# Expert results summed by an accumulating scatter into four arrays, and a combine that reads four rows per token

## The reference

```python
TOP_K = 8
shared = jax.nn.silu(xf @ Ws_up) @ Ws_down
aff = xf @ centroids.T                        # 64 experts
_, idx = jax.lax.top_k(aff + expert_biases, TOP_K)
w = jax.nn.sigmoid(jnp.take_along_axis(aff, idx, axis=1))
w = w / (jnp.sum(w, axis=-1, keepdims=True) + 1e-08)
cw = jnp.zeros((T, E)).at[jnp.arange(T)[:, None], idx].add(w)
h = jax.nn.silu(jnp.einsum('td,edf->etf', xf, W_up))
y = jnp.einsum('etf,efd->etd', h, W_down)
routed = jnp.einsum('etd,te->td', y, cw)
x = x + jnp.tanh(g_ffn[1]) * (shared + routed)
```

## Time and profile before

| | |
|---|---|
| median of 3 runs | 2478.97 us (2478.11 to 2480.88) |
| the profiled execution | 2478.53 us |
| its span | 2476.8 us |
| PE, DVE, ACT, POOL busy | 96%, 65%, 64%, 29% of the span |
| expert tiles (first to last scatter issued) | 2056.3 to 2424.0 us |
| results read back and summed | 2389.1 us to the end |

### The profile page before, as it was taken

One profiled execution on the slowest core, in us unless ns is written; L12 is line 12 of the kernel. 1 busy time (PEld: TensorE's weight loads), 2 busy tenths in 40 slices (PEclk: granted clock), 3 DMA queues, 4 the chain that ended last, 5 costly groups with the idle time before them and its releaser, 6 DMA issues. The chain is left out here.

```text
span 2476.8 us, 63160 instructions
## 1 busy us (share of the span) xinstructions
PE 2375.4 (96%) x19886; PEld 1804.3 (73%) x19887; DVE 1608.7 (65%) x5036; ACT 1583.1 (64%) x4814; POOL 728.8 (29%) x870
## 2 busy tenths in 40 slices
PE   7999999999998999999999999999999969999996
PEld 5788778778776566666666666666766648888885
DVE  4777777777774466776776767766667763333338
ACT  2777777777774566666666665665665637777770
POOL 2000000000000023233232232332332346777771
PEclk8999999999999999999999999999999989999999
DMA  5111111111111411111111111111111166776679
GB/s 160 39 44 47 45 42 47 45 42 47 47 35 36 137 30 43 34 43 43 37 43 39 40 43 35 44 43 31 49 41 32 38 181 194 215 218 209 208 265 381
DMA packets 145298, 210.14 MB, mean 85 GB/s; under 512 B 23977, under 2 KB 108507, under 8 KB 145027
## 3 DMA queue, kind: packets, MB, share of 16 engines
q1 hardware_dynamic: 114322, 139.92, 18.8%
q0 software_dynamic: 26544, 60.21, 7.3%
q10 hardware_dynamic: 4160, 6.55, 0.7%
HBM read 118.21 MB, written 96.75 MB: 87 GB/s over the span
## 5 line engine op out<-in xcount | busy, mean ns | idle before, releaser
L1456 ACT ACTIVATE wup<-bank,nmax 112x375 f32<-112x375 f32 x512 | 296.7, 585 | 110.7 <-DVE nmax L1564 109.5
L767 ACT ACTIVATE prob<-bank,nmax 112x375 f32<-112x375 f32 x512 | 291.5, 578 | 66.6 <-DVE nmax L845 62.5
L845 DVE TENSOR_REDUCE nmax<-bank 112x1 f32<-112x375 f32 x512 | 254.9, 539 | 68.7 <-PE bank L589 68.7
L1909 POOL DMA_INDIRECT expert_rows<-rows,ids x248 | 237.2, 957 | 154.2 <-ACT wup L1456 107.2
L1564 DVE TENSOR_REDUCE nmax<-bank 112x1 f32<-112x375 f32 x512 | 255.3, 541 | 20.3 <-PE bank L1252 20.1
L1315 PE MATMUL bank<-wup,wk 128*128 128x375 f32 x512 | 219.9, 512 | 2.2 <-DMA wup<-context_turned 1.0
L1021 POOL TENSOR_TENSOR stats<-stats,neg_half 112x1 f32<-112x1 f32 x64 | 35.1, 549 | 618.0 <-DVE stats L875 613.9
L1462 ACT COPY pT<-bank 128x336 f32<-128x336 f32 x512 | 201.4, 451 | 19.2 <-PE bank L1259 18.9
L1876 POOL TENSOR_TENSOR stats<-stats,neg_half 112x1 f32<-112x1 f32 x64 | 35.7, 557 | 564.9 <-DVE stats L1595 562.6
L596 PE MATMUL bank<-ident,prob 112*128 112x112 f32 x1536 | 197.2, 263 | 2.7 <-ACT prob L767 1.3
L1252 PE MATMUL bank<-wup 64*112 64x375 f32 x1024 | 194.6, 498 | 3.3 <-ACT wup L1456 3.3
(11 more groups left out here) (284 smaller groups left out, 5280.0 us busy)
## 6 DMA issues: line engine op xcount, KB each, us to landing
xr<-expert_rows SPq DMA_DIRECT2D x274, 129.0 KB
wup<-expert_results SPq DMA_DIRECT2D x14, 1024.0 KB, 17.9
wdn<-expert_results SPq DMA_DIRECT2D x14, 1024.0 KB, 20.6
wdn<-in_L_ffn_W_down_dram SPq DMA_DIRECT2D x8, 1024.0 KB, 12.4
expert_rows<-nowhere SPq DMA_DIRECT2D x56, 129.0 KB, 2.8
x_and_h_in<-stage SPq DMA_DIRECT2D x32, 224.0 KB, 2.5
xt<-x_and_h_in SPq DMA_DIRECT2D x32, 224.0 KB, 2.8
context_turned<-ctxT SPq DMA_DIRECT2D x32, 187.5 KB, 2.2
```

The lines of the kernel that those rows point to most:

```text
L767: nc.scalar.activation(prob[:, n % RING, :NK], s_bank[r][:NQ, :NK], ACT.Exp, bias=nmax[:, r:r + 1], accum_out=rsum[:, par, h:h + 1]).then_ ...
L845: nc.vector.tensor_reduce(nmax[:, r:r + 1], s_bank[r][:NQ, :NK], AX, ALU.max, negate=True).then_inc(maxed, 1)
L1456: nc.scalar.activation(prob[:, n % RING, :NK], s_bank[r][:NQ, :NK], ACT.Exp, bias=nmax[:, r:r + 1], accum_out=rsum[:, par, n:n + 1]).then_ ...
L1909: nc.gpsimd.indirect_dma_start(rows_d, bass.IndirectOffsetOnAxis(ap=ids[:, k:k + 1], axis=0), rows[:, k, :], None).then_inc(scattered, 16)
```

## The change

Results are no longer kept apart. There are four arrays `sums_d[0..3]`, each with a row of 256 values for each token and 128 spare rows behind them. POOL's scatter of tile n adds its rows to those of array n % 4 (`compute_op=ALU.add`), in the DMA engines. Array 0 starts as the residual sum (`store` in layer 1 writes it there), arrays 1 to 3 are zeroed from the tile `nowhere` by SP in layer 0 (`zero_sums`, three transfers of 112 KB for each sequence). The destination number is the token's own number. Rows that belong to nobody were dropped by a bounds check; now their number is cut by a minimum to a spare row, a different one for each partition (`padded_to`), so that all 128 rows of every tile are written. Since two scatters into one array may meet in one row, POOL waits before the scatter of tile n for the one of tile n - 4. The combine loads, for six groups of four tokens and two of two, one piece from each array (32 loads), DVE adds them (24 additions), and ACT stores eight pieces.

```diff
@@ layer0_phase, SP @@
+                def zero_sums(i):
+
+                    for c in range(1, SUMS):
+                        sp.dma_start(sums_d[c][bass.ds(i * NQ, NQ), :], nowhere[:NQ, :D]).then_inc(zeroed, 16)
...
                     if not first:
                         store(i - 1)
+                    zero_sums(i)
...
@@ layer1_phase @@
-                    sp.dma_start(seq(x3_d, p), x3[:]).then_inc(x3_out, 16)
+                    sp.dma_start(sums_d[0][p * NQ:(p + 1) * NQ, :], x3[:]).then_inc(x3_out, 16)
...
@@ expert_phase, SP @@
-                        if g % 2 == 0 and g // 2 < OWN // GROUP:
-                            sp.dma_start(x3[:, g // 2, :RUN], x3_rows[:, g // 2]).then_inc(x3_here, 16)
...
-                for n in range(OWN):
-                    if n >= GOT:
-                        by, done = summed_by(n - GOT)
-                        sp.wait_ge(by, done)
-                    sp.dma_start(got[n % GOT][:, :, :RUN], results[:, n]).then_inc(arrived[n % GOT], 16)
+                for n, (first, tokens) in enumerate(CHUNKS):
+                    for c in range(SUMS):
+                        sp.dma_start(sums_of(n, c // 2)[:, c % 2, :], planes[c][:, first * D:(first + tokens) * D]).then_inc(arrived[n][c // 2], 16)
@@ expert_phase, POOL @@
                 for n in range(N):
                     pool.wait_ge(res_made, n + 1)
-                    nc.gpsimd.indirect_dma_start(results_d, bass.IndirectOffsetOnAxis(ap=dest[:, n % DEST:n % DEST + 1], axis=0),
-                                                 res[n % RES], None, bounds_check=results_d.shape[0] - 1,
-                                                 oob_is_err=False).then_inc(res_out[n % RES], 16)
+                    if n >= SUMS:
+                        pool.wait_ge(res_out[(n - SUMS) % RES], 16 * ((n - SUMS) // RES + 1))
+                    nc.gpsimd.indirect_dma_start(sums_d[n % SUMS], bass.IndirectOffsetOnAxis(ap=dest[:, n % DEST:n % DEST + 1], axis=0),
+                                                 res[n % RES], None, compute_op=ALU.add).then_inc(res_out[n % RES], 16)
@@ expert_phase, DVE @@
-                    nc.vector.tensor_tensor(dest[:, b % DEST:b % DEST + 1], rows_of(n, b)[:, D:D + 1], beyond[:, bass.ds(n, 1)], ALU.add)
+                    nc.vector.tensor_scalar(dest[:, b % DEST:b % DEST + 1], rows_of(n, b)[:, D:D + 1], beyond[:, bass.ds(n, 1)],
+                                            padded_to[:, 0:1], ALU.add, ALU.min)
...
+                for n in range(len(CHUNKS)):
+                    for h in range(2):
+                        two = sums_of(n, h)
+                        dve.wait_ge(arrived[n][h], 32)
+                        nc.vector.tensor_tensor(two[:, 0, :], two[:, 0, :], two[:, 1, :], ALU.add).then_inc(summed, 1)
+                    one, other = sums_of(n, 0)[:, 0, :], sums_of(n, 1)[:, 0, :]
+                    dve.wait_ge(summed, 2 * n + 2)
+                    nc.vector.tensor_tensor(one, one, other, ALU.add).then_inc(added, 1)
```

More of the change, by code:

```diff
@@ L21 @@
 RESULTS = 8
+SUMS = 4
 ORDER_A = [
@@ L421, in _, with layer0_phase @@
                 dve.wait_ge(scaled, 6 + CC)
-def layer0_phase(nc, t, w, bank, arriving, x1pre_d, ctxT_d, rows_d):
+def layer0_phase(nc, t, w, bank, arriving, x1pre_d, ctxT_d, rows_d, sums_d):
     x, ctx = t["x"], t["ctx_512"]
@@ L492, in layer0_phase @@
         CAP, _ = experts_shape(t)
-        nowhere, nowhere_made, cleared = sb("nowhere", [P, D + 2]), sem("nowhere_made"), sem("cleared")
+        nowhere, nowhere_made, cleared, zeroed = sb("nowhere", [P, D + 2]), sem("nowhere_made"), sem("cleared"), sem("zeroed")
         assert E == 2 * NB
@@ L573, in _ @@
                 sp.wait_ge(cleared, 16 * (E - 8))
+                sp.wait_ge(zeroed, 16 * NB * (SUMS - 1))
                 sp.wait_ge(stored, 16 * NB)
@@ L1889, in fill @@
                     if not (isinstance(p, int) and p == 0):
-                        nc.gpsimd.tensor_scalar(rows[:, :, D], rows[:, :, D], float(NQ * TOP_K), None, ALU.add).then_inc(renumbered, 1)
+                        nc.gpsimd.tensor_scalar(rows[:, :, D], rows[:, :, D], float(NQ), None, ALU.add).then_inc(renumbered, 1)
                 def weighted_rows(p):
@@ L1921, in after @@
                     fill(p)
-                nc.gpsimd.iota(numbers[:], pattern=[[1, TOP_K]], base=0, channel_multiplier=TOP_K).then_inc(numbered, 1)
+                nc.gpsimd.iota(numbers[:], pattern=[[0, TOP_K]], base=0, channel_multiplier=1).then_inc(numbered, 1)
                 pool.wait_ge(numbered, 1)
@@ L1943, in _ @@
                 pool.wait_ge(kept_rows, p + 1)
-                nc.gpsimd.tensor_scalar(rows_last[:, :, D], rows[:, :, D], float(NQ * TOP_K), None, ALU.add).then_inc(renumbered, 1)
+                nc.gpsimd.tensor_scalar(rows_last[:, :, D], rows[:, :, D], float(NQ), None, ALU.add).then_inc(renumbered, 1)
                 pool.wait_ge(renumbered, p)
@@ L1952, in _, with expert_phase @@
                 pool.wait_ge(scattered, 16 * TOP_K * NB)
-def expert_phase(nc, t, w, bank, rows_d, results_d, x3_d, out, table, beyond, all_landed, wup, wdn):
+def expert_phase(nc, t, w, bank, rows_d, sums_d, out, table, beyond, all_landed, wup, wdn):
     NB, NQ, D = t["x"].shape
@@ L1998, in expert_phase, with sums_of @@
         RUN, GAP = 4 * D, 8
-        GROUP = RUN // D
-        assert OWN * P == NB * NQ and OWN % GROUP == 0 and TOP_K * D == 2 * RUN
+        CHUNKS = [(n, 4) for n in range(0, OWN - 4, 4)] + [(OWN - 4, 2), (OWN - 2, 2)]
+        assert OWN * P == NB * NQ and OWN % 4 == 0
         in_wup, in_wdn = pieces(wup), pieces(wdn)
         EACH = E * D // (2 * (RUN + GAP))
[L2003 to L2009, removed]
-        nothing = sb("nothing", [P, RES])
[L2012 to L2026, removed]
+        whole = [of([P, 2, RUN + GAP]) for of in (in_wup, in_wdn) for _ in range(EACH)]
+        assert len(whole) >= OWN // 4 * 2
+        def sums_of(n, half):
+            first, tokens = CHUNKS[n]
+            at = first % 4 * D
+            return whole[first // 4 * 2 + half][:, :, at:at + tokens * D]
+        arrived = [[sem(f"arrived{n}_{h}") for h in range(2)] for n in range(len(CHUNKS))]
+        summed, added, written = sem("summed"), sem("added"), sem("written")
+        padded_to, padded_known = sb("padded_to", [P, 1]), sem("padded_known")
+        padded_i = es.enter_context(nc.sbuf_tensor("padded_i", [P, 1], I32))
+        nothing = sb("nothing", [P, RES])
+        planes = [s[0:NB * NQ, :].rearrange("(p t) d -> p (t d)", p=P) for s in sums_d]
+        groups = "b q d -> (b q) d"
+        out_rows = out.rearrange(groups).rearrange("(p t) d -> p (t d)", p=P)
         def tiles(body):
@@ L2071, in _ @@
                     load(n, n % TURN)
[L2072 to L2075, removed]
-                        if g % 2 == 0 and g // 2 < OWN // GROUP:
-                            sp.dma_start(x3[:, g // 2, :RUN], x3_rows[:, g // 2]).then_inc(x3_here, 16)
+                    if n % TURN == TURN - 1 and n // TURN < N - LATE:
+                        load_late(LATE + n // TURN)
                 landed = sp.value_load(all_landed[0:1, 0:1], min_val=TOP_K * NB * NQ // P + RES, max_val=N + RES)
                 sp.wait_ge(res_made, landed)
-                for n in range(OWN):
-                    if n >= GOT:
-                        by, done = summed_by(n - GOT)
-                        sp.wait_ge(by, done)
-                    sp.dma_start(got[n % GOT][:, :, :RUN], results[:, n]).then_inc(arrived[n % GOT], 16)
+                for n, (first, tokens) in enumerate(CHUNKS):
+                    for c in range(SUMS):
+                        sp.dma_start(sums_of(n, c // 2)[:, c % 2, :], planes[c][:, first * D:(first + tokens) * D]).then_inc(arrived[n][c // 2], 16)
             @block.gpsimd
             def _(pool):
+                nc.gpsimd.iota(padded_i[:], pattern=[[0, 1]], base=NB * NQ, channel_multiplier=1).then_inc(padded_known, 1)
+                pool.wait_ge(padded_known, 1)
+                nc.gpsimd.tensor_copy(padded_to[:], padded_i[:]).then_inc(padded_known, 1)
                 for n in range(N):
                     pool.wait_ge(res_made, n + 1)
-                    nc.gpsimd.indirect_dma_start(results_d, bass.IndirectOffsetOnAxis(ap=dest[:, n % DEST:n % DEST + 1], axis=0),
-                                                 res[n % RES], None, bounds_check=results_d.shape[0] - 1,
-                                                 oob_is_err=False).then_inc(res_out[n % RES], 16)
+                    if n >= SUMS:
+                        pool.wait_ge(res_out[(n - SUMS) % RES], 16 * ((n - SUMS) // RES + 1))
+                    nc.gpsimd.indirect_dma_start(sums_d[n % SUMS], bass.IndirectOffsetOnAxis(ap=dest[:, n % DEST:n % DEST + 1], axis=0),
+                                                 res[n % RES], None, compute_op=ALU.add).then_inc(res_out[n % RES], 16)
                 for b in range(RES):
@@ L2158, in _ @@
                 pe.wait_ge(xT_out, N)
```

(14 more changed lines are left out.)

3 lines of the change are left out of this document (2 added, 1 removed).

## The result

The changed kernel takes 2615.31 us (median of 4 runs, 2612.22 to 2617.38) against 2479.48 for the kernel before: a ratio of 1.0547, interval 1.0528 to 1.0565. The forecast was 2463 us with a range up to 2550. It is 136 us slower, and the profiled span grew by 133.7 us, from 2476.8 to 2610.5 us.

The account below looks back on a forecast made before the run. POOL's descriptor making was taken to pace the expert tiles and bytes to bound the combine: 2476.8 - 20.5 (combine) + 5 (POOL's instruction) = 2461.3 us of span, + 2.2 = 2463 us; range 2446 to 2550 us.

Parts of the forecast that it names:

- POOL's instruction: Expert tiles: describing a second read per row against dropping the bounds check; pace 1.30 us for 1.281, +5 us.
- a sign of being wrong: Expert tiles: the prediction is wrong if POOL needs over 1.06 us to describe an accumulating scatter.
- landings: Slower rival, expert tiles: the scatter's landing sets POOL's pace; 2528 us at a 6.2 us landing, 2567 at 6.8; chance 0.30.
- The bounds check: POOL's scatter of 128 rows: 960 ns without the check, 973 with it; dropping it could give -4.7 us over 260 tiles.
- The new wait: POOL's wait for the scatter four tiles earlier: landing 4.4 us after its start, inside 5.2, so cost 0.
- The DMA engines: Expert tiles: 0.604 us per accumulating tile plus 0.527 for loads, 1.13 us of work per 1.30, share 0.87.
- second slower rival: Expert tiles: the DMA engines become the bound with 1.377 us of work per tile, 2490 us; chance 0.14.
- The combine: From SP's first load of sums to the end: 45.0 + 16.9 + 5.3 = 67.2 us for 87.7, -20.5 us.
- the same terms: The combine's terms with plain rows for the empty tiles: 45.0 + 10.0 + 5.3 us.
- Covered: Combine: DVE's additions, some 26 us, hidden because DVE is free from tile work before the last third of the loads.
- Layers 0 and 1: Layer 0: 96 zeroing transfers on SP, 1 us per sequence, cost 0 (32 us without cover); layer 1 issues what it did.

Follow-up runs that it names:

- e1: The changed kernel with plain scatters in place of accumulating ones, so the adding is left out: 2453.65 us, 0.9888 of the kernel before.
- e2: The changed kernel with eight arrays for the scatters and the wait on the scatter eight tiles earlier; the combine still reads four: 2613.95 us.
- e3: The changed kernel with the bounds check back and without the minimum, so rows of nobody are dropped again: 2606.72 us, 1.051 of the kernel before.
- e9: The kernel before with expert results rounded to bfloat16, combine loads of half the bytes and PE summing two tokens of three: 2449.24 us, 0.9867 of before.
- e6: The changed kernel scattering only the first 128 of each row's 256 values, into narrow arrays that the combine does not read: 2605.13 us.

## Why the prediction was wrong

**What bounds the kernel.** Right: POOL's descriptor making paces the tiles, and bytes bound the combine. This is why the error on POOL counts in full, 260 times before the combine starts.

**POOL's instruction: the step that failed.** The prediction bounded the second read of an accumulating row by half as much again as the slope over rows, 72 ns, and took 1.30 us for the pace. The instruction measured 1.551 us, a pace of 1.856: 0.575 us more than before, times 260 is 150 us, against +5 in the sum. It is also past the 1.06 us that the prediction named as a sign of being wrong. The bound held only the part that grows with rows, and even that was taken too small (2.3 to 2.7 ns per row, where 1.1 and half as much again make 1.7). That the form could have a fixed price of its own, here 0.4 us or more, had no place in it; nothing in the trace excluded one, and with another form of an instruction on the bounding engine, the fixed part is the one to leave open. The chances did give 0.44 to a slower kernel, but by landings or by full DMA engines; that POOL's own instruction would do it was no rival. The end of the range (2550) was set by landings alone, so it was too low.

**The bounds check.** Taken at 13 ns; e1 has 0.972 us without it and before had 0.973 with it. L1046's 0.960 us was another transfer, and the difference was not the check's. The prediction's lowest pace, 1.263 us, rested on it, and so did the 1.26 us expected in e1.

**The new wait: right in the tiles, with the size off.** Predicted landing 4.4 us from the start, measured 4.85, and the cost there is nothing, as forecast. Part of that is luck: the slack comes from the slow pace. At a pace of 1.28 us four of them leave 5.1, the landings in the chain go up to 5.1, and in e1 even plain scatters met three gaps in the tiles, one of them by name ended by a landing. In the combine, with the DMA engines full, the wait held POOL for 5.8 us, which the prediction didn't look at; it stayed off the path (e2).

**The DMA engines.** Predicted 0.604 us per tile for an accumulating row (0.358 to 0.850), measured 1.09 in the tiles, above the upper bound: there the old row's read and the write cost more than one of SP's loads and one plain scatter, in packets of about one row each. By the halving of the Trainium skill (Collectives: The Full Stack, "The bandwidth ceiling") it would have been 0.716; the measurement, three times the plain scatter's cost per MB, decides. Together with the loads it makes 0.90 x 1.856 = 1.67 us of DMA work per tile, more than before's pace of 1.281. So with a POOL that described accumulates for no more than plain scatters, the second slower rival would probably have come true; no run here had such a POOL, so that is only argued.

**The combine: the mechanism right, the size off.** Predicted 67.2 us, measured 72.4, with the DMA share at 1.07 from 2538.1 to 2605.4 us. With plain rows (e1) the same terms, 60.3 us, met 59.0. The accumulating alone thus cost 13.4 us here, where the prediction had 6.9 above plain rows. POOL's queue from 2538.1 to 2605.4 us says the same:

```profile
q0 software_dynamic: 4073, 3.70, 34.4%
```

That is 0.344 x 67.3 = 23.2 us of all engines for the 28 empty tiles, where 16.9 stood in the sum, or 0.83 us per tile: less than the 1.09 of the tiles, and inside the bounds of 10.0 to 23.8. "Covered", said of DVE, was nearly wrong: its additions begin when the last empty tile has left it, at 2576 us in the changed kernel. In e3 and e9 that is the end of the chain.

**Layers 0 and 1.** Right: the first expert scatter starts at 2054.2 us, 2.1 earlier than before, with 96 more transfers on SP; in the runs above it starts between 2054.2 and 2058.5 us.

What stays open is why the accumulating form has its fixed 0.4 to 0.5 us; a profile shows only that the time is in POOL's instruction.

## What to carry to other kernels

Before work is moved into a transfer, look at which engine describes the transfers and whether it sets the pace: here an add that no engine executes cost 0.58 us of POOL for each of 260 tiles, and saved 0.06 us of combine for each. When a new form of an instruction goes onto the bounding engine, measure it alone, fixed part and slope (two row counts do), before the kernel is rebuilt round it. Where a stage is bound by bytes, a narrower type gets the gain of fewer rows without a new mechanism, at the price of a rounding.

## What the runs showed of the hardware

- An accumulating indirect scatter costs POOL about 1.23 us and 2.3 to 2.7 ns per row, a plain one about 0.73 to 0.83 us and 1.1 to 1.9 ns (two different scatters), both whatever the bytes per row (e6: 512 bytes, 1.551 us; e9: 512 bytes, 0.972 us).
- On the DMA engines the accumulate of a 1 KB row costs 132.7 engine-us per MB beside the tiles' loads, the plain one 43.7. Beside the combine's loads it is 100 (0.344 x 16 x 67.3 / 3.70).
- POOL's scatter instruction gets longer in the stretch in which DVE makes its wide additions. A piece of POOL's timeline in e3_bounds, where they begin at 2574.23 us:

```profile
2571.15 1.55 POOL L2091 DMA_INDIRECT sums<-wv,dest  x1 [0.30 <-issue]
2573.01 1.55 POOL L2091 DMA_INDIRECT sums<-wv,dest  x1 [0.30 <-DMA sums<-wk,dest]
2574.86 2.01 POOL L2091 DMA_INDIRECT sums<-wv,dest  x1 [0.30 <-issue]
2577.18 2.09 POOL L2091 DMA_INDIRECT sums<-wv,dest  x1 [0.30 <-issue]
```

  In e9_bf16 some plain ones go from 0.97 to 1.39 or 1.50 us when the additions begin. Full DMA engines alone don't do it: in the changed kernel the instruction keeps its 1.55 us until 2576 us with the engines full, and has 1.97 to 2.09 us for most scatters behind it. The two stretches (busy us of PE, PEld, DVE, ACT, POOL; clock; DMA share; GB/s):

```profile
2538.10:2576.00 37.90, 24.62 (x130) 20.21 (x129) 9.82 (x33) 15.05 (x49) 27.42 (x19) 0.86 1.08 325
2576.00:2605.40 29.40, 3.22 (x16) 1.97 (x14) 24.02 (x24) 2.87 (x8) 18.37 (x10) 0.61 1.06 328
```

  It coincides with the additions in every run looked at, but ACT's stores of the output begin with them, and no run separates the two.
